# Attention stage of a one-layer language model block: q, k, v products in three f32r terms, and new orders of work on five engines

## Chip, cores and metric

The kernel runs on one core of a Trainium2 chip. The metric is device time in microseconds. Before the change it takes 3895.12 us, the median of three runs (3893.07 to 3898.6). The profiled execution took 3882.32 us, with a span of 3880.6 us from its first to its last instruction.

## What is computed

32 sequences of 512 tokens, width 256. Each token's row is an embedding plus a low-rank (LoRA) term. Then attention with 16 heads of 16: a local part (keys at most 64 positions away) and a global part (the first 64 keys), mixed by a gate. Then a mixture of 8 experts, two per token, with a capacity.

```python
h = take(emb, x) + 2.0 * take(lora_A.T, x) @ lora_B.T
n = layernorm(h)
q, k, v = split(n @ Wqkv + bqkv)              # 16 heads of 16
local  = softmax(q k^T / 4, |i - j| <= 64) v
glob   = softmax(q k[:64]^T / 4) v[:64]
gate   = sigmoid(n @ Wg + bg)
h = h + ((1 - gate) * local + gate * glob) @ Wout + bout
m = layernorm(h)                              # router, top 2 of 8, capacity
h = h + m + sum_k p_k * (silu(m @ w1[e_k]) @ w2[e_k])
```

The kernel computes the products for q, k and v in f32, and cuts q and k into bf16 terms for the scores.

## The kernel before

The kernel has a setup, an attention stage and an expert stage. The change lies in the setup and in the attention stage.

In the attention stage five engines each work through a list of their own, written out by hand as `ORDER["pe"]`, `["act"]`, `["dve"]`, `["pool"]` and `["sp"]`. An entry is (which sequence, stage, argument). The list of an engine is run once for each iteration i; "cur" is sequence i, "prev", "past" and "old" are i-1, i-2 and i-3, "nxt", "far" and "next" i+1, i+2 and i+3 (`REL`). So stages of five or six sequences lie between each other. Each engine works strictly in the order of its list; a stage begins by waiting for the semaphores of the stages whose results it needs. The small stages share two PSUM banks (`psX`), handed on in the order of TensorE's list (`take`): a stage waits until the reader of the last use of its bank is done.

The stages that matter here, of one sequence:

- "gather" 0 to 7 (POOL): eight indirect DMAs, alternately LoRA rows `la` (L582) and embedding rows `emb_t` (L585), 128 rows each. "scatter" 0 to 7 (POOL): eight indirect DMAs that write tokens' entries into the slot table (L592). These sixteen are all of POOL's indirect DMAs in a sequence.
- "scale1" (DVE) makes the normalized rows `xn`. "xn_t" 0, 1 (PE, L852) transposes them, four transposes each; ACT copies them to `xn_t` (L946).
- "qk" 0 to 3 (PE, L858): the products of `wqk` and `xn_t`, 512 columns, for two halves of the width. Each f32 matmul of the program is two instructions in the trace. ACT takes bf16 term one out of PSUM (L957), DVE the rest (L1123), ACT term two (L973), POOL term three ("qk3", L608).
- "qk_write" (SP) writes the terms to a scratch in DRAM, repeated; "load" 0 to 3 (SP, L658) brings a quarter of Q and K back, 4 heads at a time.
- "values" 0, 1 (PE, L795) and 2 (L800): the products for V of all tokens, and of the first 64.
- "max" 0 to 19 (PE, L699 to L721): scores against keys, whose row maxima DVE takes (L993, L997). There is one pair of PSUM banks for it, so max m+1 waits for DVE's reduction of max m. "m_rows", "m_out", "m_in" bring the maxima back as rows of Q.
- "exp" 0 to 19 (PE, L741, L748): the scores again, transposed; ACT takes exp (L903, L907). Also one pair of banks. "sel" (POOL, L568, L570) sets to zero what lies outside the band, for 16 of the 20.
- "out" (PE, L769, L774): probabilities times V; "evac" (ACT, L913); "mix" (PE transposes L817, DVE L1089 and L1096, POOL L601); "attn_t"; "project"; the second layernorm, the router and the ranks.
- "hold" (POOL, L620) adds the output bias to h; SP stores it and "hb" (SP, L662) loads it again.

In POOL's list of before, several indirect DMAs follow each other: `("next", "gather", 1), ("past", "scatter", 2), ("next", "gather", 2), ("next", "gather", 3), ("past", "scatter", 3), ("next", "gather", 4)` is one run, and there are three pairs.

## Time and profile before

| | |
|---|---|
| median of three runs | 3895.12 us |
| profiled execution | 3882.32 us, span 3880.6 us |
| mean granted TensorE clock | 0.952 |
| PE busy in the span | 3481.5 us (90%) |
| POOL busy | 2324.1 us (60%) |
| DVE busy | 2172.5 us (56%) |
| ACT busy | 1868.3 us (48%) |
| chain that ended last | PE 40%, all of it in the expert stage (L1462, L1497, L1437) |

PE is TensorE, with its weight loads apart (PEld); DVE is VectorE, ACT ScalarE, POOL GpSimd, SP the engine that issues most DMAs (its queue is SPq). L12 is line 12 of the kernel. A busy share is a mean over stages with different limits, so the windows of a stage say more. "PEclk" is the granted TensorE clock in a stretch, as a share of 2.4 GHz. In a timeline an entry in brackets is the idle time of the engine before the group, and what ended it: "issue" is time in which the engine waited for nothing that the profile shows, "remote" an event that none of the profiled engines gave. Durations of single matmuls contain the depth of their pipeline; how far apart they start is their cost in a row.

### The profile page before, as it was taken

To read this page: it belongs to the slowest core of one execution; us is meant where nothing else is said; L and a number is where in the kernel's file an instruction comes from. 1 tells how busy PE (TensorE), PEld (TensorE's weight loads), DVE (VectorE), ACT (ScalarE), POOL (GpSimd) and SP (SyncE) were. 2 spreads that over 40 slices of the span, in tenths; PEclk is the share of its full clock that TensorE was granted. 3 is DMA by queue.
4 is the path that set the end of the run, shared out by engine and by line. 5 is a ranking of instruction groups with operands and counts; after the bars stand their busy time and mean duration, and the time that the engine had idled before them with its cause. 6 is when DMAs were issued, how large, how long until landed. Compare 5 with 4: busy or idle time off the path is not lost. (4 is left out here: it accounts for less than half of the span.)

```text
span 3880.6 us, 117579 instructions
## 1 busy us (share of the span) xinstructions
PE 3481.5 (90%) x47537; PEld 2753.0 (71%) x47537; DVE 2172.5 (56%) x5392; ACT 1868.3 (48%) x3086; POOL 2324.1 (60%) x2599
## 2 busy tenths in 40 slices
PE   2898889888888888888899849999999999999998
PEld 1555555555555555555555539999999999999998
DVE  3576767767676776767677634343434344443333
ACT  0455555555555555555555624343444444444343
POOL 5566777777777777777776645444544444444443
PEclk7899999999999999999999969999999999999999
DMA  4354544445454444545454323232323233222222
GB/s 142 123 157 117 163 122 151 130 138 139 128 152 123 150 133 135 144 125 149 124 154 130 109 87 65 50 68 46 71 48 72 48 69 72 46 51 45 45 45 41
DMA packets 242540, 398.31 MB, mean 103 GB/s; under 512 B 34572, under 2 KB 150748, under 8 KB 242044
## 3 DMA queue, kind: packets, MB, share of 16 engines
q1 hardware_dynamic: 168540, 297.43, 25.0%
q0 software_dynamic: 70512, 91.16, 13.8%
q8 instruction: 345, 5.65, 0.6%
q10 hardware_dynamic: 3008, 2.95, 0.2%
q14 instruction: 135, 1.11, 0.1%
HBM read 198.55 MB, written 192.88 MB: 101 GB/s over the span
## 5 line engine op out<-in xcount | busy, mean ns | idle before, releaser
L1388 POOL DMA_INDIRECT out_y<-out_t,tok_out x264 | 425.7, 1612 | 747.3 <-DMA out_y<-out_t,tok_out 405.0
L1534 ACT ACTIVATE act<-psS 128x512 f32<-128x512 f32 x528 | 316.9, 600 | 882.1 <-PE psS L1462 880.9
L1596 DVE TENSOR_TENSOR h_lo<-act,h_hi 128x512 fp32r<-128x512 f32 x528 | 367.2, 695 | 562.3 <-ACT h_hi L1535 543.8
L993 DVE TENSOR_REDUCE negm<-psS 128x4 f32<-128x640 f32 x512 | 418.8, 818 | 452.3 <-remote 276.3
L903 ACT ACTIVATE pl<-psS 128x896 f32<-128x896 f32 x512 | 467.7, 913 | 379.9 <-PE psS L741 372.0
L568 POOL TENSOR_SCALAR_AFFINE_SELECT pl<-pl 128x512 f32<-128x512 f32 x512 | 354.3, 692 | 448.4 <-ACT pl L903 446.2
L1497 PE MATMUL psO<-w_hi,h_hi 128*128 128x256 f32 x2112 | 598.8, 284 | 0.8 <-DVE h_lo L1596 0.8
L1497 PE MATMUL psO<-w_lo,h_hi 128*128 128x256 f32 x2112 | 588.7, 279 | 0.0
L1497 PE MATMUL psO<-w_hi,h_lo 128*128 128x256 f32 x2112 | 587.6, 278 | 0.0
L1462 PE MATMUL psS<-xg_hi,w_hi 128*128 128x256 f32 x1984 | 551.7, 278 | 0.0
L1462 PE MATMUL psS<-xg_hi,w_lo 128*128 128x256 f32 x1984 | 551.5, 278 | 0.0
L1462 PE MATMUL psS<-xg_lo,w_hi 128*128 128x256 f32 x1984 | 551.3, 278 | 0.0
L1497 PEld LDWEIGHTS psO<-w_hi,h_hi 128*128 128x128 f32 x2112 | 397.0, 188 | 1.1 <-DVE h_lo L1596 1.0
L1497 PEld LDWEIGHTS psO<-w_lo,h_hi 128*128 128x128 f32 x2112 | 397.0, 188 | 0.0
L1497 PEld LDWEIGHTS psO<-w_hi,h_lo 128*128 128x128 f32 x2112 | 395.5, 187 | 0.0
L1462 PEld LDWEIGHTS psS<-xg_hi,w_hi 128*128 128x128 f32 x1984 | 375.1, 189 | 0.0
L1462 PEld LDWEIGHTS psS<-xg_lo,w_hi 128*128 128x128 f32 x1984 | 372.5, 188 | 0.0
L1462 PEld LDWEIGHTS psS<-xg_hi,w_lo 128*128 128x128 f32 x1984 | 372.4, 188 | 0.0
L699 PE MATMUL psS<-K,Q 96*32 96x160 bf16 (+2 forms) x8192 | 260.8, 237 | 105.7 <-DVE negm L993 71.2
L1628 DVE TENSOR_SCALAR out_t<-psO,wt_all 128x256 f32<-128x256 f32 x264 | 127.8, 484 | 360.7 <-PE psO L1497 355.8
L699 PEld LDWEIGHTS psS<-K,Q 96*32 96x32 bf16 x8192 | 165.6, 98 | 231.2 <-DVE negm L993 109.0
L570 POOL TENSOR_SCALAR_AFFINE_SELECT pl<-pl 128x512 f32<-128x512 f32 x512 | 328.0, 641 | 0.0
(232 smaller groups left out, 7728.6 us busy)
## 6 DMA issues: line engine op xcount, KB each, us to landing
qk_scr<-qk SPq DMA_DIRECT2D x64, 768.0 KB
Q<-qk_scr SPq DMA_DIRECT2D x128, 384.0 KB
K<-qk_scr SPq DMA_DIRECT2D x128, 384.0 KB
qk_scr<-qk SPq DMA_DIRECT2D x64, 512.0 KB
qk_scr<-qk SPq DMA_DIRECT2D x64, 256.0 KB
h_rows<-held SPq DMA_DIRECT2D x32, 512.0 KB
hb<-h_rows SPq DMA_DIRECT2D x32, 512.0 KB
x_rows<-x SPq DMA_DIRECT2D x32, 512.0 KB
```

The lines of the kernel that those rows point to most:

```text
L568: pool.affine_select(out=cols[:, :, 0:P], in_=cols[:, :, 0:P], compare_op=ALU.is_ge, fill=0.0, base=0, pattern=[[0, 4], [1, P]], channel_m ...
L570: pool.affine_select(out=cols[:, :, P:WIN], in_=cols[:, :, P:WIN], compare_op=ALU.is_ge, fill=0.0, base=0, pattern=[[0, 4], [-1, P]], chan ...
L699: pe.matmul(psS[SUB * c:SUB * (c + 1), 2 + a, q % 2 * BAND + lo:q % 2 * BAND + hi], Q[0:ROWS, 4 * g + 2 * v + a, (4 * q + c) * SUB:(4 * q ...
L903: act.activation(pl[:, v, half, :, lo:hi], psS[:, 0:2, lo:hi], ACT.Exp, scale=SCALE).then_inc(exp_done, 1)
L993: dve.tensor_reduce(negm[:, g, 0, v, :, 2 * half:2 * half + 2], psS[:, 2:4, 0:2 * BAND].rearrange("p a (q u) -> p a q u", u=BAND), AX.X, A ...
L1388: pool.indirect_dma_start(out=y[:, :], in_=out_t[:, tile.out, s, :], in_offset=None, out_offset=bass.IndirectOffsetOnAxis(ap=tok_out[:, ti ...
L1462: last = pe.matmul(psS[:, f // 2, (f % 2) * 256:(f % 2) * 256 + cols], w[:, tile.par, k, fs], x[:, k, 0:cols], start=(k == 0 and n == 0), ...
L1497: last = pe.matmul(psO[:, s, 0:D], h_[:, f, ts], w[:, tile.par, f, :], start=(f == 0 and n == 0), stop=(f == FT - 1 and n == 2))
L1534: act.activation(act32[:, b, :, 0:cols], src, ACT.Silu)
L1596: dve.tensor_tensor(h_lo[:, 2 * b:2 * b + 2, 0:cols], act32[:, b, :, 0:cols], h_hi[:, 2 * b:2 * b + 2, 0:cols].bitcast(F32), ALU.subtract) ...
L1628: dve.tensor_scalar(out_t[:, tile.out, s, :], psO[:, s, 0:D], wt_all[:, bass.ds(tile.h0 + s, 1)], None, ALU.mult).then_inc(out_done, 1)
```

## The change

1. The f32 products of q, k and v become sums of three f32r products: the operands are cut into a high part and the rest, and hi x hi, hi x lo and lo x hi are added up in PSUM. The weights are cut in the setup, by DVE. The transposed rows are cut for each sequence: ACT copies the high part out of PSUM, and a new stage "xn_lo" on DVE subtracts it from the PSUM tile. The bank is given free by DVE instead of ACT. "values" and "qk" wait for the low part.
2. The tiles of the cut rows have 64 columns more, a second copy of the first 64 tokens, so that values 2 is one product of 128 columns of tokens and 256 columns of weights instead of two half ones.
3. All five lists are written anew. In POOL's no two indirect DMAs follow each other, also not from one iteration to the next. The sixteen per sequence stay.

```diff
-        wv_sb = keep("wv_sb", [P, KT, D])
+        wv_hi = keep("wv_hi", [P, KT, D], F32R)
+        wv_lo = keep("wv_lo", [P, KT, D], F32R)
...
-        wqk = keep("wqk", [P, KT, 4, P])
+        wqk_hi = keep("wqk_hi", [P, KT, 4, P], F32R)
+        wqk_lo = keep("wqk_lo", [P, KT, 4, P], F32R)
...
+                    dve.tensor_copy(wv_hi[:, :, :], wv_raw[:, :, :])
                     for k in range(KT):
                         for s in range(2):
-                            dve.tensor_copy(wqk[:, k, 2 * s:2 * s + 2, :].rearrange("p a (d h) -> p a d h", d=HD),
-                                            wqk_raw[:, k, s * D:(s + 1) * D].rearrange("p (h a d) -> p a d h", a=2, d=HD))
+                            ins = dve.tensor_copy(wqk_hi[:, k, 2 * s:2 * s + 2, :].rearrange("p a (d h) -> p a d h", d=HD),
+                                                  wqk_raw[:, k, s * D:(s + 1) * D].rearrange("p (h a d) -> p a d h", a=2, d=HD))
+                    ins.then_inc(w_cut, 1)
+                    dve.wait_ge(w_cut, 1)
+                    dve.tensor_tensor(wv_lo[:, :, :], wv_raw[:, :, :], wv_hi[:, :, :].bitcast(F32), ALU.subtract)
+                    for k in range(KT):
+                        for s in range(2):
+                            dve.tensor_tensor(wqk_lo[:, k, 2 * s:2 * s + 2, :].rearrange("p a (d h) -> p a d h", d=HD),
+                                              wqk_raw[:, k, s * D:(s + 1) * D].rearrange("p (h a d) -> p a d h", a=2, d=HD),
+                                              wqk_hi[:, k, 2 * s:2 * s + 2, :].rearrange("p a (d h) -> p a d h", d=HD).bitcast(F32),
+                                              ALU.subtract)
...
-            xn_t = tmp("xn_t", [P, KT, T])
+            xn_hi = tmp("xn_hi", [P, KT, SIDE + T], F32R)
+            xn_lo = tmp("xn_lo", [P, KT, SIDE + T], F32R)
...
             ORDER["pe"] = (
...
-                ("nxt", "max", 9), ("nxt", "values", 0), ("nxt", "max", 10), ("prev", "logits", None), ("cur", "exp", 19),
-                ("nxt", "values", 1), ("cur", "out", 10), ("cur", "out", 11), ("nxt", "m_rows", 1), ("nxt", "values", 2),
-                ("nxt", "max", 11), ("far", "xn_t", 0), ("far", "xn_t", 1), ("nxt", "exp", 0), ("nxt", "max", 12), ("far", "qk", 0),
-                ("nxt", "exp", 1), ("far", "qk", 1), ("far", "qk", 2), ("nxt", "max", 13), ("far", "qk", 3), ("nxt", "exp", 2),
...
+                ("cur", "exp", 18), ("prev", "router", None), ("nxt", "max", 9), ("nxt", "values", 0), ("cur", "exp", 19),
+                ("nxt", "values", 1), ("cur", "out", 10), ("cur", "out", 11), ("prev", "logits", None), ("nxt", "m_rows", 1),
+                ("nxt", "max", 10), ("nxt", "values", 2), ("far", "xn_t", 0), ("far", "xn_t", 1), ("nxt", "exp", 0),
+                ("nxt", "max", 11), ("nxt", "exp", 1), ("far", "qk", 0), ("nxt", "max", 12), ("far", "qk", 1), ("nxt", "max", 13),
+                ("nxt", "exp", 2), ("far", "qk", 2), ("nxt", "max", 14), ("far", "qk", 3), ("nxt", "exp", 3), ("nxt", "max", 15),
+                ("cur", "mix", 0), ("nxt", "max", 16), ("nxt", "exp", 4), ("cur", "mix", 1), ("nxt", "out", 0), ("nxt", "max", 17),
+                ("nxt", "m_rows", 2), ("nxt", "exp", 5), ("cur", "mix", 2), ("nxt", "max", 18), ("nxt", "exp", 6),
+                ("nxt", "out", 1), ("nxt", "max", 19), ("nxt", "exp", 7), ("cur", "mix", 3), ("nxt", "exp", 8), ("nxt", "out", 2),
+                ("nxt", "out", 3), ("nxt", "exp", 9), ("prev", "ahead", None), ("cur", "attn_t", 0), ("far", "max", 0),
...
             ORDER["dve"] = (
...
+                ("nxt", "qk", 0), ("cur", "max", 13), ("nxt", "qk", 1), ("cur", "max", 14), ("nxt", "qk", 2),
...
+                ("past", "top", 6), ("far", "scale1", 3), ("nxt", "max", 10), ("far", "xn_lo", 0), ("far", "xn_lo", 1),
+                ("prev", "top", 0), ("nxt", "max", 11), ("prev", "top", 1), ("nxt", "max", 12),
...
             ORDER["pool"] = (
-                ("nxt", "hold", 0), ("far", "gather", 5), ("cur", "sel", 0), ("cur", "sel", 1), ("nxt", "hold", 1),
-                ("nxt", "qk3", 0), ("nxt", "qk3", 1), ("nxt", "qk3", 2), ("nxt", "qk3", 3), ("cur", "sel", 2), ("prev", "mix", 0),
-                ("cur", "sel", 3), ("old", "scatter", 4), ("old", "scatter", 5), ("prev", "mix", 1), ("cur", "sel", 5),
-                ("cur", "sel", 6), ("prev", "mix", 2), ("prev", "mix", 3), ("far", "gather", 6), ("cur", "sel", 7),
-                ("nxt", "hold", 2), ("cur", "sel", 8), ("far", "gather", 7), ("old", "scatter", 6), ("nxt", "hold", 3),
-                ("cur", "sel", 10), ("old", "scatter", 7), ("cur", "sel", 11), ("cur", "sel", 12), ("prev", "rstd2", None),
-                ("cur", "sel", 13), ("past", "scatter", 0), ("past", "scatter", 1), ("cur", "sel", 15), ("cur", "sel", 16),
-                ("cur", "sel", 17), ("next", "gather", 0), ("far", "rstd1", None), ("cur", "sel", 18), ("next", "gather", 1),
-                ("past", "scatter", 2), ("next", "gather", 2), ("next", "gather", 3), ("past", "scatter", 3), ("next", "gather", 4),
+                ("far", "gather", 4), ("nxt", "hold", 2), ("nxt", "hold", 3), ("far", "gather", 5), ("cur", "sel", 0),
+                ("old", "scatter", 0), ("cur", "sel", 1), ("far", "gather", 6), ("cur", "sel", 2), ("nxt", "qk3", 0),
+                ("nxt", "qk3", 1), ("nxt", "qk3", 2), ("nxt", "qk3", 3), ("prev", "mix", 0), ("cur", "sel", 3),
+                ("old", "scatter", 1), ("prev", "mix", 1), ("old", "scatter", 2), ("cur", "sel", 5), ("prev", "mix", 2),
+                ("cur", "sel", 6), ("far", "gather", 7), ("prev", "mix", 3), ("old", "scatter", 3), ("cur", "sel", 7),
+                ("old", "scatter", 4), ("cur", "sel", 8), ("old", "scatter", 5), ("cur", "sel", 10), ("old", "scatter", 6),
+                ("cur", "sel", 11), ("old", "scatter", 7), ("cur", "sel", 12), ("prev", "rstd2", None), ("cur", "sel", 13),
+                ("next", "gather", 0), ("cur", "sel", 15), ("cur", "sel", 16), ("next", "gather", 1), ("cur", "sel", 17),
+                ("far", "rstd1", None), ("cur", "sel", 18), ("next", "gather", 2), ("far", "hold", 0), ("next", "gather", 3),
+                ("far", "hold", 1),
...
             ORDER["sp"] = (
-                ("prev", "m_out", 3), ("cur", "load", 1), ("cur", "hold", None), ("prev", "m_in", 3), ("cur", "load", 2),
-                ("past", "x2", None), ("cur", "m_out", 0), ("cur", "m_in", 0), ("cur", "load", 3), ("cur", "m_out", 1),
-                ("nxt", "qk_write", (0, 0)), ("nxt", "qk_write", (0, 1)), ("nxt", "qk_write", (0, 2)), ("cur", "m_in", 1),
-                ("nxt", "qk_write", (1, 0)), ("nxt", "qk_write", (1, 1)), ("nxt", "qk_write", (1, 2)), ("nxt", "load", 0),
-                ("cur", "m_out", 2), ("past", "y", None), ("prev", "hb", None), ("cur", "m_in", 2),
+                ("old", "y", None), ("cur", "load", 1), ("prev", "m_out", 3), ("prev", "m_in", 3), ("cur", "m_out", 0),
+                ("cur", "load", 2), ("cur", "m_in", 0), ("nxt", "hold", None), ("prev", "hb", None), ("cur", "load", 3),
+                ("cur", "m_out", 1), ("cur", "m_in", 1), ("nxt", "qk_write", (0, 0)), ("nxt", "qk_write", (0, 1)),
+                ("past", "x2", None), ("nxt", "qk_write", (0, 2)), ("nxt", "qk_write", (1, 0)), ("nxt", "qk_write", (1, 1)),
+                ("nxt", "qk_write", (1, 2)), ("cur", "m_out", 2), ("nxt", "load", 0), ("cur", "m_in", 2),
...
-                            wv = wv_sb[:, :, :].rearrange("p k (v a d) -> p k a v d", a=2, d=HD)
-                            pe.wait_ge(xn_t_done, KT * (s + 1))
+                            pe.wait_ge(xn_lo_done, KT * (s + 1))
                             take(key, v_done, 3 * s + arg + 1)
                             if arg < 2:
                                 for j in range(2):
-                                    tok = slice((2 * arg + j) * P, (2 * arg + j + 1) * P)
+                                    tok = slice(SIDE + (2 * arg + j) * P, SIDE + (2 * arg + j + 1) * P)
                                     for k in range(KT):
-                                        last = pe.matmul(psX[:, b, j * D:(j + 1) * D], xn_t[:, k, tok], wv_sb[:, k, :],
-                                                         start=(k == 0), stop=(k == KT - 1))
+                                        for n, (x_, w) in enumerate(((xn_hi, wv_hi), (xn_hi, wv_lo), (xn_lo, wv_hi))):
+                                            last = pe.matmul(psX[:, b, j * D:(j + 1) * D], x_[:, k, tok], w[:, k, :],
+                                                             start=(k == 0 and n == 0), stop=(k == KT - 1 and n == 2))
                             else:
                                 for k in range(KT):
-                                    for a in range(2):
-                                        last = pe.matmul(psX[64 * a:64 * (a + 1), b, 0:P], xn_t[:, k, 0:64], wv[:, k, a, :, :],
-                                                         start=(k == 0), stop=(k == KT - 1))
+                                    for n, (x_, w) in enumerate(((xn_hi, wv_hi), (xn_hi, wv_lo), (xn_lo, wv_hi))):
+                                        last = pe.matmul(psX[:, b, 0:D], x_[:, k, 0:2 * SIDE], w[:, k, :],
+                                                         start=(k == 0 and n == 0), stop=(k == KT - 1 and n == 2))
...
                         if stage == "xn_t":
                             pe.wait_ge(xn_done, QB * (s + 1))
-                            take(key, xn_t_done, KT * s + arg + 1)
+                            take(key, xn_lo_done, KT * s + arg + 1)
...
                         if stage == "qk":
-                            pe.wait_ge(xn_t_done, KT * (s + 1))
+                            pe.wait_ge(xn_lo_done, KT * (s + 1))
                             take(key, qk_rest_done, 4 * s + arg + 1)
                             for k in range(KT):
-                                last = pe.matmul(psX[:, b, :], wqk[:, k, arg, :], xn_t[:, k, :],
-                                                 start=(k == 0), stop=(k == KT - 1))
+                                for n, (w, x_) in enumerate(((wqk_hi, xn_hi), (wqk_hi, xn_lo), (wqk_lo, xn_hi))):
+                                    last = pe.matmul(psX[:, b, :], w[:, k, arg, :], x_[:, k, SIDE:SIDE + T],
+                                                     start=(k == 0 and n == 0), stop=(k == KT - 1 and n == 2))
...
-                            act.activation(xn_t[:, arg, :], psX[:, b, :], ACT.Copy).then_inc(xn_t_done, 1)
+                            act.activation(xn_hi[:, arg, 0:SIDE], psX[:, b, 0:SIDE], ACT.Copy)
+                            act.activation(xn_hi[:, arg, SIDE:SIDE + T], psX[:, b, :], ACT.Copy).then_inc(xn_hi_done, 1)
...
+                        if stage == "xn_lo":
+                            dve.wait_ge(xn_hi_done, KT * s + arg + 1)
+                            if arg == 0:
+                                need(dve, v_ready, 3 * s)
+                                need(dve, qk_ready, 4 * s)
+                            x_ = psX[:, BANK["xn_t", arg, s], :]
+                            dve.tensor_tensor(xn_lo[:, arg, 0:SIDE], x_[:, 0:SIDE], xn_hi[:, arg, 0:SIDE].bitcast(F32), ALU.subtract)
+                            dve.tensor_tensor(xn_lo[:, arg, SIDE:SIDE + T], x_, xn_hi[:, arg, SIDE:SIDE + T].bitcast(F32),
+                                              ALU.subtract).then_inc(xn_lo_done, 1)
```

## Rows read from the trace of the kernel before

**Rows 1.** windows by stage: us; busy PE, PEld, DVE, ACT, POOL; clock; DMA share, GB/s.

```profile
333.20:2091.60 1758.40, 1559.27 (x27784) 971.25 (x27773) 1225.34 (x3300) 966.21 (x1506) 1270.18 (x1637) 0.95 0.48 138
2400.00:3880.00 1480.00, 1450.81 (x12479) 1448.68 (x12477) 594.26 (x1169) 627.73 (x1150) 686.30 (x521) 0.99 0.30 54
```

**Rows 2.** DMA issues of one tile: count, durations, first and last start.

```profile
L662 SPq DMA_DIRECT2D hb<-h_rows x11: 441/452/2097, 1012.4 to 1688.7; - x11
...
L668 SPq DMA_DIRECT2D x_rows<-x x32: 360/376/381, 225.2 to 2265.0; - x32
```

**Rows 3.** timeline of PE, from 1109 us: start, duration, line, operation, [idle before].

```profile
1109.92 0.46 PE L699 MATMUL psS<-K,Q 96*32 96x96 bf16 x16
...
1110.43 0.33 PE L878 MATMUL psX<-ident,score_t 128*128 128x128 f32 x1
...
1115.19 0.66 PE L800 MATMUL psX<-wv_sb,xn_t 128*64 128x128 f32 x8
...
1117.99 0.24 PE L715 MATMUL psS<-mask,identb 128*32 128x128 bf16 x2 [1.16 <-issue]
...
1120.85 1.08 PE L852 MATMUL psX<-ident,xn 128*128 128x128 f32 x4 [0.96 <-issue]
```

**Rows 4.** timeline of POOL, first and last of a run of six indirect DMAs.

```profile
1112.33 1.03 POOL L585 DMA_INDIRECT emb_t<-in_L_tok_emb_weight,id_cur  x1 [0.18 <-issue]
...
1118.86 0.98 POOL L582 DMA_INDIRECT la<-lora_rows,id_cur  x1 [0.30 <-issue]
```

**Rows 5.** timelines of DVE and ACT, the first work behind that run.

```profile
1122.47 0.83 DVE L993 TENSOR_REDUCE negm<-psS 128x4 f32<-128x640 f32 x1 [7.96 <-remote]
...
1120.15 0.56 ACT L924 ACTIVATE V<-psX 64x128 f32<-64x128 f32 x2 [2.96 <-remote]
```

**Rows 6.** a window at 1124 us, and PE's timeline of the q,k products.

```profile
1124.20:1127.80 3.60, 3.60 (x13) 1.24 (x13) 0.82 (x1) 0.70 (x2) 1.22 (x2) 0.54 0.00 0
...
1124.21 3.60 PE L858 MATMUL psX<-xn_t,wqk 128*128 128x512 f32 x4
...
1128.13 3.70 PE L858 MATMUL psX<-xn_t,wqk 128*128 128x512 f32 x8
```

**Rows 7.** timelines of POOL and PE around two of the pairs.

```profile
1100.47 0.98 POOL L592 DMA_INDIRECT slot_table<-entry,slot_i  x1 [0.30 <-issue]
...
1100.24 0.45 PE L699 MATMUL psS<-K,Q 96*32 96x160 bf16 x15
...
1101.99 1.06 PE L774 MATMUL psO<-pg,V 128*32 128x512 f32 x8
...
1156.85 0.46 PE L699 MATMUL psS<-K,Q 96*32 96x96 bf16 x16 [1.06 <-DVE negm L993]
```

**Rows 8.** timelines of POOL and PE, two single DMAs, the last q,k, the first max.

```profile
1108.81 1.02 POOL L582 DMA_INDIRECT la<-lora_rows,id_cur  x1 [0.28 <-POOL id_cur L577]
...
1148.92 0.99 POOL L582 DMA_INDIRECT la<-lora_rows,id_cur  x1
...
1132.26 1.98 PE L858 MATMUL psX<-xn_t,wqk 128*128 128x512 f32 x4
...
1150.67 0.46 PE L699 MATMUL psS<-K,Q 96*32 96x96 bf16 x16 [0.52 <-DMA K<-qk_scr]
```

**Rows 9.** timeline of PE, a values group.

```profile
1108.02 1.97 PE L795 MATMUL psX<-wv_sb,xn_t 128*128 128x256 f32 x8
```

**Rows 10.** groups by line, 1000 to 1700 us, and DVE's timeline in the setup.

```profile
L1144 DVE TENSOR_TENSOR h<-psX,hb 128x512 f32<-128x512 f32 x20 | 13.6, 680 | 0.0
...
L924 ACT ACTIVATE V<-psX 64x128 f32<-64x128 f32 x20 | 5.5, 273 | 20.7 <-remote 20.6
...
42.09 1.26 DVE L316 COPY wqk<-wqk_raw 128x256 f32<-128x256 f32 x4
```

**Rows 11.** groups by line, whole run: count, busy, mean ns, idle before.

```profile
L769 PE MATMUL psO<-pl,V 128*32 128x256 f32 x2048 | 184.2, 385 | 6.2 <-POOL pl L570 2.5 <-issue 1.5
...
L699 PE MATMUL psS<-K,Q 96*32 96x96 bf16 x1024 | 136.3, 212 | 68.2 <-DVE negm L993 43.9 <-DMA K<-qk_scr 15.9 <-issue 7.0
```

More of the change, by code:

```diff
@@ L481, in build @@
-                ("nxt", "exp", 1), ("far", "qk", 1), ("far", "qk", 2), ("nxt", "max", 13), ("far", "qk", 3), ("nxt", "exp", 2),
-                ("nxt", "max", 14), ("cur", "mix", 0), ("nxt", "exp", 3), ("nxt", "out", 0), ("nxt", "max", 15), ("cur", "mix", 1),
-                ("nxt", "exp", 4), ("nxt", "max", 16), ("cur", "mix", 2), ("nxt", "exp", 5), ("nxt", "max", 17), ("nxt", "out", 1),
-                ("nxt", "m_rows", 2), ("nxt", "exp", 6), ("nxt", "max", 18), ("cur", "mix", 3), ("nxt", "exp", 7),
@@ L485, in build @@
-                ("nxt", "max", 19), ("nxt", "out", 2), ("nxt", "exp", 8), ("nxt", "out", 3), ("prev", "ahead", None),
-                ("cur", "attn_t", 0), ("far", "max", 0), ("cur", "attn_t", 1), ("nxt", "m_rows", 3), ("nxt", "exp", 9),
+                ("cur", "exp", 11), ("prev", "project", 1), ("nxt", "max", 3), ("cur", "out", 4), ("cur", "exp", 12),
+                ("far", "embed", None), ("nxt", "max", 4), ("cur", "exp", 13), ("cur", "out", 5), ("far", "lora", 0),
+                ("cur", "exp", 14), ("far", "lora", 1), ("nxt", "max", 5), ("cur", "out", 6), ("cur", "exp", 15), ("cur", "out", 7),
@@ L520, in build @@
-                ("prev", "top", 6), ("far", "max", 4), ("next", "lora", 0), ("far", "cut", (0, 0)), ("cur", "scale2", 0),
+                ("nxt", "qk", 0), ("cur", "max", 13), ("nxt", "qk", 1), ("cur", "max", 14), ("nxt", "qk", 2),
+                ("cur", "cut", (2, 0)), ("nxt", "qk", 3), ("cur", "max", 15), ("cur", "cut", (2, 1)), ("prev", "mix", (0, 0)),
+                ("cur", "cut", (2, 2)), ("prev", "mix", (0, 1)), ("cur", "cut", (2, 3)), ("past", "top", 2), ("cur", "max", 16),
+                ("prev", "mix", (1, 0)), ("prev", "mix", (1, 1)), ("past", "top", 3), ("cur", "max", 17), ("cur", "kg", 2),
@@ new lines, in build @@
+                ("past", "top", 4), ("cur", "kg", 3), ("prev", "mix", (2, 0)), ("cur", "max", 18), ("prev", "mix", (2, 1)),
+                ("nxt", "zgate", 0), ("old", "rank", 5), ("prev", "mix", (3, 0)), ("prev", "mix", (3, 1)), ("cur", "max", 19),
+                ("cur", "cut", (3, 0)), ("cur", "cut", (3, 1)), ("far", "la_cut", 0), ("cur", "cut", (3, 2)), ("past", "rank", 0),
+                ("cur", "cut", (3, 3)), ("nxt", "max", 0), ("past", "rank", 1), ("past", "rank", 2), ("far", "la_cut", 1),
```

68 lines of the change are left out of this document (30 added, 38 removed).

## The prediction, made before the change was run

> **What bounds the kernel now.** I read the windows by stage first, then one sequence's timeline on each engine. The windows part the 90% for which TensorE (PE) is busy into two stages [rows 1]: the expert stage from 2400 us on, where PE is busy 1450.8 of 1480 us at clock 0.99 and which the change doesn't touch, and the attention stage, where PE is busy 88.7% at clock 0.95, GpSimd (POOL) 72%, VectorE (DVE) 70%, ScalarE (ACT) 55%. The whole gain or loss is made in attention. There one sequence takes 67.6 us: ten repeats of one DMA lie between 1012.4 and 1688.7; over all 32 the same kind of count gives (2265.0 - 225.2)/31 = 65.8 [rows 2], the ends being thinner.
>
> In this loop PE is the fullest engine, but it isn't full. Reading its timeline from 1115 us [rows 3]: the groups from values 2 (1115.19) to the first q,k product (1124.21) take 9.0 us. They are values 2, two max groups, two sets of transposes and one score group. A max group undisturbed takes 0.5 (1109.92 to 1110.43, first two rows); by sizes I put the others at 0.6, 0.6, 0.6 and 0.4, 3.2 in all. So 5.8 us are lost, in gaps called "issue" even inside the max group, where nothing is waited for. At that time POOL runs six indirect DMAs with nothing between them, 1112.33 to 1119.84, and a seventh after one addition [rows 4]. DVE's next max begins at 1122.47 after 7.96 us idle, though its matmuls ended by 1118.23; ACT sat 2.96 us until 1120.15 with its input done at about 1115.9; both are put down to "remote", no engine's event [rows 5]. So while indirect DMAs follow each other, signals between the other engines arrive late, for all of them at once.
>
> The idle time also costs clock. From 1124.20 to 1127.80 the granted clock is 0.54, that is nearly all at the lower level of 1.2 GHz, after PE had been half idle for 5 us; four q,k instructions then take 3.53 us, and eight at 1.00 take 3.70 [rows 6]. Lost: 3.53 - 1.77 = 1.8 us. The mean 0.95 of the stage says that it happens in each sequence.
>
> Pairs do the same on a small scale [rows 7]: beside the second DMA at 1100.47 a max group runs from 1100.24 to 1101.99, 1.75 for 0.5, lost 1.2. Of the other two pairs one costs a wait of 1.06 (at 1156.85) and the last, read in the same way, about 0.3. DMAs that stand alone: three besides the seventh. Beside the one at 1108.81 PE loses nothing (its values group of 1108.02 takes 1.97 us, as the other one does), beside that of 1148.92 it waits 0.52 [rows 8, 9], the third costs about 0.2. Sum per sequence: 5.8 + 1.8 for the run, 2.6 for three pairs, 0.7 for three single ones.
>
> **The change part by part.**
>
> *Product passes.* Each f32 matmul is two instructions. Sixteen for q,k at (3.70 - 0.16)/8 = 0.44, the 0.16 being the tail of the last, 7.1 us at full clock; for values 16 at 1.97/8 = 0.246, 3.9 us, and 0.6 for values 2 [rows 6, 9]. After: 24 f32r instructions of 512 columns for q,k, 24 of 256 columns for values 0 and 1, 6 of 256 for values 2. The expert stage gives f32r with 256 columns: 12479 instructions in 1450.8 us, 0.116 each [rows 1], so 0.23 for 512 at most and 0.21 if part of the 0.116 is fixed; I take 0.22: 5.3, 2.8 and 0.7, with 0.1 to start each of seven groups 9.5 us against 11.6. Saved 2.1 us; the ends are 1.7 and 2.8 (no start cost). I take 2.5, nearer the upper end, since the groups of before carry their start cost too.
>
> *Extra cuts.* ACT copies two times 64 columns more; nearest row 0.27 (64x128), 0.5 us on an engine 55% busy: no cost. DVE gets two subtractions of 128x512 out of PSUM, like 0.68, and two of 64 columns, 0.2 each, at most the 0.27 of the ACT row [rows 10]: 1.8 us on DVE, 47.1 to 48.9 us busy, still under PE. What costs is latency: q,k now waits for transposes, ACT and DVE in a row. From the last transpose: 0.6 + 0.2 on ACT, 0.7 + 0.2 on DVE, some 0.1 of signals, 1.8 us; PE has a score, a max and a score group of 1.3 us between. I take 0.5 us of waiting, ends 0 and 1.9 (no cover). Behind the subtractions DVE holds max 11, so PE's max 12 is next in danger, but q,k work of PE lies before it. The PSUM bank of the transposes comes free later by the same time; inside the 0.5.
>
> *The lists.* The order changes on all five engines; the same 16 indirect DMAs per sequence now always have a sel, a mix or another POOL operation between them. This takes away the run and the pairs: 5.8 + 1.8 + 2.6 = 10.2, and with the 0.7 of the single ones 10.9. It adds 16 single ones. Their price is the crux: the trace has 0, 0.5 and 0.2, and half a pair is 0.43. I take 0.35, 5.6 us; ends 0 and 0.65 (a DMA of 1.0 us and some 0.4 behind it, until PE and DVE start again [rows 5, 7], make 1.4 in which a signal is late by 0.7 on average, felt nearly in full). On POOL the gap before a DMA goes from 0.30 behind a DMA to 0.18 behind a sel, nothing on the path. With no long idle left the clock should stay up.
>
> *Moved DMAs.* SP's q,k writes and loads keep their order, y and hold move to the other side of the loads. PE's wait for K at the first max of a quarter is 15.9 us over all 32 sequences, 0.5 each [rows 11]. Between q,k 3 and max 0 PE's new list holds twelve score and max groups of about 0.45 and eight mix and output groups of about 1, some 14 us with the small ones; now 16.4 pass there (1134.2 to 1150.67 [rows 8]), and the wait at the end is 0.52. With the delays of five single DMAs and the earlier start of q,k 0 it comes out about even. Cost 0 to 1.5, taken 0, since y moved out of its way.
>
> *Setup.* DVE gets a copy of 128x512, a subtraction of that size and four of 128x256 strided; like copies take 1.26/4 = 0.3 each [rows 10]: 3 us, in the open, as POOL's first gathers begin only after DVE's last. Ends 1.5 and 4.
>
> Sum: 67.6 - 10.9 + 5.6 - 2.5 + 0.5 = 60.3 us a sequence, 7.3 less. 26 full periods give 190; the five thinner intervals at the ends, at half, 18; setup -3: 205 us. The profiled execution took 3882.3 us (span 3880.6 and 1.7 around it) and would take 3677; the median shown, 3895.1, lies 12.8 above it, so 3690.
>
> *A rule against it.* ACT and DVE are held while POOL issues indirect DMAs [rows 4, 5]. The Trainium skill, "SBUF — State Buffer", section "SBUF: two separate sides", says that engine ports and DMA ports are disjoint, and that PE, ACT and DVE's own ports never wait on anyone; only DVE and GpSimd share a lock. By it a run of DMAs delays no other engine, the waits have another source, and new lists bring nothing: a rival, below. The rows speak against it by coincidence in time, which isn't yet cause.
>
> **The rivals.**
>
> *Single ones are nearly free* (0.05 each). For: 1108.81. Then 60.3 - 4.8 = 55.5 us, 12.1 less: 26 x 12.1 + 30 - 3 = 342, and 3553. Against: POOL needs about 49 us busy and 16 x 0.2 of gaps in 55.5, in order; it would become the bound at about 57, which gives 3590.
>
> *The delay is the DMAs' in sum, or isn't theirs.* If each single costs 0.65, the loop is 65.1; if only the passes count, 67.6 - 2.5 + 0.5 = 65.6. Saved 2.2: 26 x 2.2 + 6 - 3 = 60, and 3835. For: each DMA is still issued and the traffic (DMA share 0.48) stays. Against: delays of 5 us at the run and 1 at a pair, on three engines.
>
> *POOL's order becomes the bound, slower.* Some twelve DMAs that ran in bunches now stand between sels, and each pushes the next sel back by 1.17 us. PE's output group waits for sel, ACT's exp for the output group's release. If these waits are felt in full, 12 x 1.17 = 14.0, and the loop is 67.6 - 10.9 - 2.5 + 0.5 + 14.0 = 68.7; that is 1.1 x 28.5 + 3 = 34 slower, 3930. It decides once PE waits for pl from POOL at nearly every output group. Against: that wait is 2.5 us in all now [rows 11], POOL has 19 us idle a sequence.
>
> **How the numbers follow.** Forecast 0.52 (own range 3620 to 3760: singles 0.15 to 0.5, passes 1.7 to 2.8), singles free 0.20, in sum or not theirs 0.19, slower 0.09, of which 0.01 within 0.2% of before, which is about what this kernel's measurement can tell from no change. Hence faster 0.91, same 0.01, slower 0.08. Predicted 3690; the range 3580 to 3840 takes in the first rival at POOL's bound and the middle of the second.
>
> **What would show it.** Right: a sequence in 58 to 63 us; no idle of DVE over 2 us put down to "remote"; granted clock about 1.00 in attention; q,k instructions 0.22 apart; PE waits of 0 to 0.6 near single DMAs. Wrong: clock still 0.95; waits of over 2 us with no DMA behind another; POOL idle under 4 us a sequence with PE waiting for pl; DVE's waits for the new cut over 1 us.

## The result: 87 us faster where 205 were forecast

The changed kernel takes 3806.7 us (3804.0 to 3807.8) against 3894.1 (3884.0 to 3898.6): ratio 0.9778, 95% interval 0.9758 to 0.9798. The forecast was 3690, range 3580 to 3840.

The windows of the changed kernel (us; busy PE, PEld, DVE, ACT, POOL; clock; DMA share, GB/s), to be set beside [rows 1]:

```profile
333.00:2050.00 1717.00, 1482.93 (x28561) 1035.89 (x28557) 1296.36 (x3449) 983.97 (x1575) 1294.30 (x1659) 0.94 0.47 142
2310.00:3790.00 1480.00, 1463.81 (x12612) 1461.76 (x12611) 598.21 (x1177) 634.62 (x1163) 690.39 (x525) 1.00 0.30 55
```

PE is busy 86.4% of attention, less than before, and the clock is 0.94, not 1.00. The repeats of one DMA, as in [rows 2]:

```profile
L680 SPq DMA_DIRECT2D hb<-h_rows x11: 446/453/1726, 1022.9 to 1671.1; - x11
...
L686 SPq DMA_DIRECT2D x_rows<-x x32: 359/1041/2654, 255.5 to 2195.3; - x32
```

A full sequence takes 64.8 us instead of 67.6, where 60.3 were forecast; over all 32 it is 62.6 instead of 65.8. What DVE's maxima waited for, of the kernel before (total us, times):

```profile
  remote: 276.3, 57
  PE psS L715: 175.9, 173
```

and of the changed one:

```profile
  PE psS L733: 183.3, 206
  PE psS L739: 16.3, 36
```

As forecast, none of DVE's idle before its maxima is called "remote" any more; shorter delays are left and are measured below. But PE's groups by line, as in [rows 11], have a wait for K that was 15.9 us before (line L699 there) and is 84.9 now, 13.4 and 13.6 of it a single wait at the start:

```profile
L717 PE MATMUL psS<-K,Q 96*32 96x160 bf16 (+2 forms) x8192 | 262.6, 239 | 105.2 <-DMA K<-qk_scr 84.9 <-DVE negm L1013 14.1 <-DVE negm L1017 1.2
```

DVE waits for the last gather of the sequence two ahead (waits by line: total, times, longest):

```profile
DVE la_four L1189 <- DMA emb_t<-in_L_tok_emb_weight,id_cur: 141.0, 32, 12.9
```

One sequence's timeline shows both waits meeting:

```profile
1096.73 0.39 PE L877 MATMUL psX<-xn_hi,wqk_lo 128*128 128x512 f32 x1
...
1110.58 0.32 SPq L676 DMA_DIRECT2D Q<-qk_scr  x1
1110.95 0.71 SPq L676 DMA_DIRECT2D K<-qk_scr  x1
1111.18 1.00 POOL L603 DMA_INDIRECT emb_t<-in_L_tok_emb_weight,id_cur  x1 [0.15 <-issue]
...
1116.18 0.73 PE L717 MATMUL psS<-K,Q 96*32 96x96 bf16 x16 [2.53 <-DMA K<-qk_scr]
1116.64 0.63 DVE L1189 CAST la_four<-la 128x128 fp32r<-128x128 f32 x1 [3.65 <-DMA emb_t<-in_L_tok_emb_weight,id_cur]
...
1118.03 1.09 PE L842 MATMUL psX<-ident,attn 128*128 128x128 f32 x4 [0.92 <-DVE ahead L1076]
1119.15 0.60 ACT L955 ACTIVATE attn_t<-psX 128x512 f32<-128x512 f32 x1 [4.38 <-issue]
...
1120.76 2.94 PE L849 MATMUL psX<-wout_sb,attn_t 128*128 128x256 f32 x8
```

The last q,k product ends at 1097.1 (first row). Load 0 is issued 13.5 us later, and max 0 starts 19.1 later; before, max 0 started 16.4 behind that product [rows 8]. SP's list accounts for a part of the first: m load 1 now stands ahead of the q,k writes and waits for its own write, the residual's store stands among them:

```profile
1096.92 0.26 SPq L657 DMA_DIRECT2D Q<-m_scr  x1
1097.37 0.92 SPq L667 DMA_DIRECT2D qk_scr<-qk  x2
1098.33 1.07 SPq L686 DMA_DIRECT2D x_rows<-x  x1
1099.44 5.44 SPq L667 DMA_DIRECT2D qk_scr<-qk  x4
```

SP's waits for such a write of m, of the kernel before and of the changed one (total, times, longest):

```profile
SPq L639 <- DMA m_scr<-m_t: 113.0, 59, 4.4
```

```profile
SPq L657 <- DMA m_scr<-m_t: 277.8, 95, 7.6
```

After these waits the clock falls, in a new place:

```profile
1110.00:1116.00 6.00, 3.17 (x37) 1.17 (x29) 2.89 (x6) 3.07 (x5) 5.49 (x8) 0.99 0.75 192
1116.00:1124.00 8.00, 6.91 (x110) 5.41 (x114) 4.62 (x17) 1.92 (x3) 4.96 (x7) 0.58 0.49 146
1118.00:1121.00 3.00, 2.97 (x51) 2.47 (x52) 1.51 (x7) 1.84 (x3) 0.92 (x1) 0.50 0.50 118
```

PE is half idle for 6 us, then the granted clock is at its lower level, 1.2 GHz.

### The profile page after: what moved, and what is told of

Same layout as the page of the kernel before. It is cut to its first block and busy times, and to the rows that moved or that the text cites. A ratio compares the mean times of both kernels' runs of the same rounds, so it can differ in the third digit from the quotient of the medians.

```text
span 3806.0 us, 118732 instructions
## 1 busy us (share of the span) xinstructions
PE 3366.0 (88%) x47985; PEld 2813.8 (74%) x47985; DVE 2243.9 (59%) x5526; ACT 1874.0 (49%) x3150; POOL 2331.6 (61%) x2599
## 5 line engine op out<-in xcount | busy, mean ns | idle before, releaser
L1417 POOL DMA_INDIRECT out_y<-out_t,tok_out x264 | 426.6, 1616 | 745.5 <-DMA out_y<-out_t,tok_out 403.2
L586 POOL TENSOR_SCALAR_AFFINE_SELECT pl<-pl 128x512 f32<-128x512 f32 x512 | 329.1, 643 | 320.3 <-ACT pl L922 316.7
L717 PE MATMUL psS<-K,Q 96*32 96x160 bf16 (+2 forms) x8192 | 262.6, 239 | 105.2 <-DMA K<-qk_scr 84.9
L588 POOL TENSOR_SCALAR_AFFINE_SELECT pl<-pl 128x512 f32<-128x512 f32 x512 | 328.5, 642 | 0.0
```

The costliest lines, as they stand in the source:

```text
L586: pool.affine_select(out=cols[:, :, 0:P], in_=cols[:, :, 0:P], compare_op=ALU.is_ge, fill=0.0, base=0, pattern=[[0, 4], [1, P]], channel_m ...
L588: pool.affine_select(out=cols[:, :, P:WIN], in_=cols[:, :, P:WIN], compare_op=ALU.is_ge, fill=0.0, base=0, pattern=[[0, 4], [-1, P]], chan ...
L717: pe.matmul(psS[SUB * c:SUB * (c + 1), 2 + a, q % 2 * BAND + lo:q % 2 * BAND + hi], Q[0:ROWS, 4 * g + 2 * v + a, (4 * q + c) * SUB:(4 * q ...
L1417: pool.indirect_dma_start(out=y[:, :], in_=out_t[:, tile.out, s, :], in_offset=None, out_offset=bass.IndirectOffsetOnAxis(ap=tok_out[:, ti ...
```

## The experiments

They ran on two groups of chips. The changed kernel, E1 to E4 and E5 to E8 met chips on which the kernel before takes 3892 to 3894 us: the *late* chips. E9 to E12 and the three sets behind them met chips on which the same kernel takes 3678, 3684 and 3681 us: the *prompt* chips. Each ratio is to the kernel before on the same chip. All the late sets were taken before the prompt ones, so whether it is the chip or the hour was not settled. The stage behind attention takes the same on both: from SP's last store of a sequence's rows (`x_rows`) to the end, the kernel before needs 1616 us in its late trace and 1619 in its prompt one, so the 209 us by which these traces differ lie ahead of it.

**E1, products alone**, in the lists of before:

```diff
+ three-term f32r products, 64 columns more
  ORDER["dve"]: ... ("nxt","max",11), ("far","xn_lo",0), ("far","xn_lo",1), ("nxt","max",12) ...
```

> The three-term products alone, in the lists of before (the two low-part stages stand on DVE behind max 11). Theory A, the passes give 2.5 us a sequence where PE is the bound but the long run of indirect DMAs still holds all engines: a sequence goes from 67.6 to about 66 us, 40 to 70 us less, 3825 to 3855; DVE's idle of 7 to 8 us put down to remote stays, clock 0.95. Theory B, the whole gain of the change was the passes and the lists give nothing: 3800 to 3815.

Measured: 3893.4, ratio 1.0002 (0.9992 to 1.0012). Both expectations missed. In the trace PE waits 0.6 us a sequence for DVE's low part; its idle called "issue" at the transposes, which now also wait for DVE's release of the bank, is 56.5 us in all where it was 30.2; DVE's maxima behind the run of six start 5.7 us late (median) where they started 4.3 late; and the clock of attention is 0.93 instead of 0.95.

**E2, the five new lists alone**, f32 products (the new lists, without "xn_lo"):

> The five new lists alone, with the f32 products of before and without the low-part stages. Theory A, spacing the DMAs removes about 9 us of waiting a sequence and a new chain, from the q,k writes over the load of K to the next first max, takes most of it back: 3840 to 3870, with PE's wait for K at 2 to 3 us a sequence. Theory B, the lists give nothing: 3885 to 3900.

Measured: 3838.2, 0.9859 (0.9830 to 0.9887), just under Theory A's range, but not by its mechanism: PE's wait for K is 22.3 us in all, 0.3 a sequence without the first wait, not 2 to 3. DVE's wait for the gather is there, 112.7 us in all. The products on top bring 31 us, to 3807.

**E3, POOL's list alone spaced**, all else as before:

```diff
-  past.scatter 0, past.scatter 1, sel 15, sel 16, sel 17, gather 0, rstd1, sel 18, gather 1, past.scatter 2, gather 2, gather 3, past.scatter 3, gather 4
+  past.scatter 0, sel 15, past.scatter 1, sel 16, gather 0, sel 17, gather 1, rstd1, past.scatter 2, sel 18, gather 2, (next) hold 0, gather 3, sel 0, old.scatter 3 ...
```

> The kernel before with POOL's list alone changed, so that no two indirect DMAs follow each other; products and the other four lists are those of before. Theory A, a run of indirect DMAs delays the signals between all engines until it ends, a single one by at most 1.5 us: the delays of 4 to 5 us at DVE's max go, none over 1.5 us is left, the low clock in each sequence goes, and a sequence takes 60 to 63 us, 3680 to 3770 in all. Theory B, the cost is that of 16 DMAs however they stand: 3870 to 3910. In between (3780 to 3860): the delays go as in A, and a chain of DMAs takes over as in the changed kernel.

Measured: 3783.1, 0.9721 (0.9701 to 0.9741). The longest delay of a maximum is 1.27 us, as Theory A had it, but the time lies above its range and the clock of attention is 0.97, not 1.00; the new wait for K of the changed kernel isn't there (13.4 us in all, 13.0 of it at the start). One list does more than the whole change. So the other four lists, with the products, cost.

**E4, gathers off POOL**, the kernel before with the eight gathers as plain DMAs from fixed rows on SP's queue (so other rows are gathered); pairs of scatters stay:

```diff
-  pool.indirect_dma_start(out=la[:, q, :], in_=lora_rows[:, :], in_offset=at)
+  sp.dma_start(la[:, q, :], lora_rows[row:row + P, :])
```

> The kernel before with the eight gathers of a sequence taken off POOL: SP issues plain DMAs of the same sizes from fixed rows instead, so the embedding rows are not those of the tokens, and the routing differs. Eight scatters stay, in four pairs. Theory A, it is POOL's indirect DMAs in a row that delay signals: the run shrinks to a pair, no delay over 2.3 us, a sequence about 60 us, attention 200 us shorter (the expert stage may differ by the routing and is left out of the comparison). Theory C, the traffic on the DMA engines delays the signals, whoever issues it: delays of 4 us stay where the gathers now stand, and attention is at most 50 us shorter.

Measured: 3639.9, 0.9354 (0.9339 to 0.9370). Attention, from the first sequence's store to the last one's, is 246 us shorter (1794 against 2040), where Theory C allowed 50. The same bytes move: the loss is not traffic. Not all of the 246 need be delays, since POOL also has eight instructions less in a sequence; E12 bears on that.

**E5, E6, E7, the two new waits**, in the changed kernel. E5 is the SP edit, E6 the DVE edit, E7 both:

```diff
-  m_out 1, m_in 1, qk_write (0,0), qk_write (0,1), x2, qk_write (0,2), (1,0), (1,1), (1,2)
+  m_out 1, qk_write (0,0), qk_write (0,1), m_in 1, qk_write (0,2), (1,0), (1,1), (1,2), x2
```

```diff
-  cut (3,1), far.la_cut 0, cut (3,2), rank 0, cut (3,3), max 0, rank 1, rank 2, far.la_cut 1
+  cut (3,1), cut (3,2), rank 0, cut (3,3), max 0, rank 1, rank 2, far.la_cut 0, far.la_cut 1
```

> The changed kernel with SyncE's list alone reordered: the layer's m load 1 goes behind the first two q,k writes, and the store of the residual behind all q,k writes. Theory A (the new period is set by a chain that the new SyncE order delays: q,k writes, then load of K): the matmuls on K wait under 1 us a sequence for it instead of 2.6, load 0 is issued 3 to 5 us earlier, and the time comes to 3740 to 3790. Rival (the K wait only shows the place where another lateness surfaces; ScalarE or VectorE bound the period): the wait moves to VectorE's or ScalarE's rows and the time stays within 0.5% of 3807.

> The changed kernel with VectorE's list alone reordered: the cut of the next sequence's gathered rows that waits 4.3 us for its gather goes behind the rank step. Theory A (period set by the K chain): VectorE's wait of 4.3 us on the gather goes, but TensorE still waits for K, so 0 to 40 us are gained: 3765 to 3807. Rival (VectorE's standing still there is what makes the period longer): 4.3 us over 25 sequences less some slack, 3710 to 3760.

> Both reorderings of the changed kernel at once (SyncE's writes ahead of m load 1 and the residual's store; VectorE's cut behind the rank step). Theory A: the two waits are one after the other in time on TensorE's path, so the gains add to more than either alone: 3690 to 3770, the half-speed stretch of each sequence gone or under 4 us. Rival (something else in the new lists holds the period): within 20 us of the better of the two alone.

Measured: E5 3802.3 (0.9769, 0.9752 to 0.9785), E6 3771.1 (0.9701, 0.9672 to 0.9730), E7 3706.9 (0.9522, 0.9507 to 0.9538). Alone 4 and 36 us, together 100: the waits overlap in time. With either left something still waits there (PE's wait for K is 52.4 us in all in E5 and 111.2 in E6; DVE's for the gather 138.3 in E5), and the clock of attention is 0.95 and 0.96. In E5 SP's waits for m's write fell from 277.8 to 94.7 us. E5 met its rival's figure, E6 and E7 Theory A's. E7's window, and its wait for K:

```profile
333.00:2050.00 1717.00, 1529.10 (x30393) 1060.35 (x30392) 1387.22 (x3659) 1047.73 (x1674) 1361.33 (x1749) 0.99 0.51 149
```

```profile
L718 PE MATMUL psS<-K,Q 96*32 96x160 bf16 (+2 forms) x8192 | 248.3, 234 | 80.7 <-DMA K<-qk_scr 47.1 <-DVE negm L1014 26.4 <-DVE negm L1018 1.2
```

Clock 0.99, and 3707 where the prediction said 3690. That agreement hides two errors of opposite sign, as the last runs show: more than forecast from the delays, nothing from the products.

**E8, products with E3's spaced list**, low part made behind max 11:

> The kernel before with the three-term products and with GpSimd's list alone spaced (SyncE, ScalarE, TensorE and VectorE lists as before, except that the low part of the normalised rows is made behind the eleventh maximum). Theory A (products are worth their shorter passes where no run of indirect DMAs stands behind them): the spaced list alone gave 3783, less 1 to 2.5 us over 32 sequences, 3700 to 3755. Rival (products give nothing in the lists of before, as alone: the extra step of VectorE for the low part takes what the passes give): 3770 to 3800.

Measured: 3803.1, 0.9762 (0.9742 to 0.9782), that is 20 us above E3. Worse than the rival's range: with POOL's list spaced and the rest as before the products cost, where in E1 they gave nothing. PE waits 38.1 us in all, 1.1 a sequence, for the low part.

**E9 to E12**, all from E7: E9 with f32 products; E10 with POOL's list bunched (`gather 1, 2, 3, 4, 5, scatter 0` in one run, scatters 1-2, 3-4, 5-6 in pairs); E11 with two moves in PE's list (m_rows 0 behind max 8, max 0 behind attn_t 1), the first followed in ACT's; E12 with gathers on SP as in E4.

> The lists of the last experiment that took 3706.9 (both reorderings), with the products of the kernel before (one f32 matmul for each pair of operands instead of three f32r ones, no low part of the rows made on VectorE). If the shorter passes of the products are worth the 2.5 us a sequence of the prediction once the waits beside them are gone: 3707 + 2.5 x 32 = 3787, say 3770 to 3800. Rival (they are worth what they gave in the new lists as they stood, 31 us, or nothing as in the lists of before): 3705 to 3745.

> The lists that took 3706.9, with GpSimd's alone changed: its indirect DMAs stand in one run of six, three pairs and four singles, as in the kernel before. Theory A (a run of six costs 7.6 us, three pairs 2.6, singles 0.35 each): 6 us a sequence more, 3870 to 3900. Rival (most of what the whole change gave came of other places in the lists, and a run costs only what the slack of TensorE doesn't take): 3720 to 3780.

> The lists that took 3706.9, with TensorE's list changed in two places: the first quarter's rows of maxima are turned behind maximum 8 (they wait 1.06 us a sequence for VectorE's cut), and maximum 0 stands behind both turns of the attention's output (it waits 1.09 us for K); ScalarE's list follows the first. If the two waits are on the path: 2 us over some 30 sequences less, 3645 to 3680. Rival (VectorE's maxima bound the period by then, so the waits come back under its name): 3695 to 3715.

> The lists that took 3706.9, with the eight gathers of a sequence taken from GpSimd and made plain DMAs from fixed rows on SyncE's queue (the rows gathered are therefore not the reference's); GpSimd keeps the eight single scatters. If singles cost 0.35 us each, as the prediction has it: 2.8 us a sequence, 3600 to 3635. Rival (singles are hidden in TensorE's slack): 3690 to 3707. Rival (SyncE's queue is late by its new DMAs): above 3710.

Measured, on a prompt chip (before 3678.4): E9 3681.8 (1.0015, 0.9998 to 1.0032), E10 3768.0 (1.0244, 1.0216 to 1.0273), E11 3670.8 (0.9981, 0.9961 to 1.0002), E12 3580.3 (0.9741, 0.9714 to 0.9768). No expected time can be read against these, as all were worked out from 3707 on a late chip. So the comparison was made again on one chip, with these expectations:

> The changed kernel again, on one chip with the three runs that follow. Two kinds of chip were met: on the first the kernel before takes 3892 to 3895 us and signals come up to 5 us late behind GpSimd's indirect DMAs; on the second it takes 3678 and they hardly do. On the first kind: ratio 0.978 again. On the second, if the gain came from the spacing of the indirect DMAs alone: the new waits (K, the gather's cut) are left, so not faster, ratio 1.00 to 1.02; rival (the gain has nothing to do with the delay): 0.97 to 0.985 there too.

> The changed kernel with both reorderings again, as the one that the next two runs are set beside. First kind of chip: 0.952 again. Second kind: the rest of its lists is level with the lists of before, 0.99 to 1.00.

> The same lists with the f32 products of before. If the shorter passes are worth 2.5 us a sequence once the two waits are gone: 1.02 times m_e7 (3787 where that is 3707). Rival (they are worth nothing to 31 us, the extra steps on VectorE taking the rest): 1.000 to 1.008 times m_e7.

> The same lists with GpSimd's indirect DMAs in one run of six, three pairs and four singles. Where signals are late behind them (first kind of chip): 6 us a sequence more, 1.043 to 1.052 times m_e7, by the prediction's terms. Second kind: only what the later gathers cost, which the one run there put at 3768 against 3671 to 3682 for lists with singles, so 1.01 to 1.03 times m_e7. Rival (the delay costs nothing in these lists): the same 1.01 to 1.03 on the first kind.

A prompt chip again (before 3683.8): the change 3770.5, ratio 1.0230 (1.0180 to 1.0281), so slower, though not surely by 2%, and above both expected ranges; E7 3683.6 (0.9997, 0.9975 to 1.0019), as expected; E9 3682.7 (0.9999, 0.9979 to 1.0020); E10 3770.8 (1.0240, 1.0189 to 1.0291). So in E7's lists the products are worth 0 (E9 against E7: the rival), and with the delays absent a bunched order can still lose: in E10 PE waits for K 4.3 us a sequence, and its ratio to E7, 1.024, lies in the range expected for prompt chips. What bunching costs E7 on a late chip wasn't measured.

**The kernel before, and E3, once more:**

> The kernel before itself, for its trace on one chip with the next run. Second kind of chip (3670 to 3690 us): VectorE's maxima start within 0.1 us of TensorE's end even beside the run of six, where they came 4.3 us late on the first kind; a sequence takes 6 to 7 us less than the 65.8 of the first. First kind: 3890 to 3900 and delays of 4 to 5 us. Ratio 1.000 either way.

> The kernel before with GpSimd's list alone spaced (no two indirect DMAs behind one another), again. If the gain of 0.972 on the first kind came of the delays behind a run: on the second kind 0.995 to 1.010. Rival (the spaced order is better by itself, whatever the signals do): 0.97 to 0.985 there too. First kind: 0.972 again.

A prompt chip (before 3681.3): 3675.5 (0.9979, 0.9953 to 1.0006) and 3713.9 (1.0100, 1.0064 to 1.0136). Both as expected for prompt chips, the second at the edge of its range. Spacing is worth 2.8% on a late chip and costs 1.0% here. What DVE's maxima wait for in the kernel before, on this chip, beside the 276.3 above:

```profile
  PE psS L715: 202.3, 193
  PE psS L721: 21.4, 28
  remote: 4.6, 2
```

and its run of six, the same code as in [rows 3 to 5]:

```profile
1142.46 0.95 POOL L585 DMA_INDIRECT emb_t<-in_L_tok_emb_weight,id_cur  x1 [0.30 <-issue]
...
1143.60 0.28 PE L715 MATMUL psS<-mask,identb 128*32 128x128 bf16 x7
1143.72 1.01 POOL L592 DMA_INDIRECT slot_table<-entry,slot_i  x1 [0.30 <-issue]
...
1143.96 0.82 DVE L993 TENSOR_REDUCE negm<-psS 128x4 f32<-128x640 f32 x1 [2.25 <-PE psS L715]
1145.03 0.98 POOL L582 DMA_INDIRECT la<-lora_rows,id_cur  x1 [0.30 <-issue]
...
1147.95 3.70 PE L858 MATMUL psX<-xn_t,wqk 128*128 128x512 f32 x8
```

DVE starts 0.08 us behind PE's last matmul (1143.60 + 0.28), beside the fifth DMA of the run; in [rows 5], also beside the fifth, it came 4.2 us late. POOL's DMAs last as long as there, and lie as close. What differs in these rows is when DVE sees PE's signal. Over the window from 400 to 2000 us it starts at most 0.2 us late beside a run of six (50 maxima).

## Why the prediction was wrong

**Each late signal's price.** Beside each kernel its time on a late and a prompt chip. Their difference is taken for what the delays cost it; that rests on two comparisons, the equal stage behind attention and the signals that are prompt in the prompt traces, and nothing else was held against it:

| | late | prompt | delays |
|---|---|---|---|
| before | 3893 | 3681 | 212 |
| E3, POOL's list spaced | 3783 | 3714 | 69 |
| the change | 3807 | 3770 | 37 |
| E7, both moves | 3707 | 3684 | 23 |

*Mechanism and run.* "Signals between the other engines arrive late" was right for PE's signals to DVE and ACT. From 400 to 2000 us, where PE's last matmul ended beside an indirect DMA or less than 0.5 us behind it, DVE's maxima start after PE's end by 4.27 us (median) at a run of six, 2.11 at a pair, 0.34 at a single in the change and 1.24 in E3, and with no DMA near by 0.04 to 0.06; ACT's exponentials by 1.39 at a pair and 0.53 at a single. The two figures for singles differ by where PE ends: within 0.25 us of the DMA's start DVE is 1.25 late (25 cases in E3), about 1.0 behind it 0.49 (48 in the change), 2.0 behind it 0.05 (16 in E3). So a signal seems to be held until some 1.5 us behind the start of the last DMA, an estimate from these three rows. On prompt chips all medians are under 0.2.

*The prices* were both too high. The prediction's 26 full periods and 5 halves are 28.5 sequences. Taking away 10.9 us in each would be 311; all delays of before cost 212, 7.4 a sequence. Singles at 5.6 would be 160; they cost 37, 0.08 each (69 in E3, 0.15). Net the term was forecast at 151 and measured at 212 - 37 = 175: within 24 us, by errors that cancel. 1108.81 [rows 8], at which PE lost nothing, was the typical one.

*The step that failed* is "Moved DMAs ... Cost 0 to 1.5, taken 0, since y moved out of its way". On prompt chips, where no delay is in play, the change is 87 us slower than before, and E7's two moves give these 87 back: 3 us a sequence. On late chips the same two moves give 100. The prediction looked at y and hold and not at m load 1 and the residual's store, which came ahead of the writes, and not at all at la_cut, which came to stand some 2 us behind its gather's issue, where the gather lands 5.5 behind it (1111.18 to 1116.64). Its upper end, 1.5, held only half of the cost. That is 87 of the 118 us that are missing. The wait for K that it took as 0.5 a sequence was misread too, for all but 2.5 us of it is one wait at the start:

```profile
PE psS L699 <- DMA K<-qk_scr: 15.9, 5, 13.4
```

```profile
PE psS L717 <- DMA K<-qk_scr: 84.9, 31, 13.6
```

The new lists have one more wait that no term had and no experiment took away: PE waits for ACT's exponentials 50.5 us in all in the change, 5.1 before.

*The second step that failed* is "Product passes ... I take 2.5". The passes did get shorter: q,k instructions start 0.23 apart (0.22 forecast). This stretch is at full clock:

```profile
1094.29 0.40 PE L877 MATMUL psX<-xn_hi,wqk_hi 128*128 128x512 f32 x1
1094.53 0.39 PE L877 MATMUL psX<-xn_lo,wqk_hi 128*128 128x512 f32 x1
1094.76 0.40 PE L877 MATMUL psX<-xn_hi,wqk_lo 128*128 128x512 f32 x1
```

But E7 and E9, on one chip, with three-term and f32 products, PE busy 1532 and 1564 of 1717 us:

```profile
333.00:2050.00 1717.00, 1532.20 (x30540) 1072.59 (x30533) 1403.23 (x3685) 1054.31 (x1690) 1369.84 (x1759) 0.97 0.51 149
```

```profile
333.00:2050.00 1717.00, 1563.98 (x30138) 1008.43 (x30137) 1372.05 (x3593) 1047.18 (x1637) 1374.86 (x1765) 0.99 0.51 149
```

and the two kernels' waits of the maxima's matmuls:

```profile
L718 PE MATMUL psS<-K,Q 96*32 96x160 bf16 (+2 forms) x8192 | 255.4, 237 | 96.8 <-DMA K<-qk_scr 74.8 <-DVE negm L1014 15.8 <-DVE negm L1018 1.5
```

```profile
L702 PE MATMUL psS<-K,Q 96*32 96x160 bf16 (+2 forms) x8192 | 247.7, 233 | 64.9 <-DVE negm L996 30.2 <-DMA K<-qk_scr 28.3 <-DVE negm L1000 1.5
```

PE's busy time fell by 1.1 us a sequence (31.8 us over the 29 sequences of the window), or by 1.8 if the time at 1.2 GHz is counted at half (1542 to 1490 us), so the passes gave nearly what was forecast, and a lower clock, 0.97 against 0.99, took 0.7 of it. The wait for K rose by 46.5 us, 1.5 a sequence: PE's work wasn't the bound there; what the shorter passes freed came out as a longer wait for K. It isn't the low part that holds K up. From the last transpose to the first q,k product pass 2.0 us in E7 and 1.9 in E9 (medians), 0.1 for the term of 0.5, and the products themselves take 8.1 instead of 9.4. But from their end to SP's load 0 pass 12.3 us instead of 9.5: the last q,k write begins 4.7 behind them instead of 3.6, and SP waits for the landing of these writes 101.3 us in all instead of 60.0. Why that stretch grew isn't shown. The prediction priced latency against PE's cover at that spot alone, not against the load at the end of the chain. Net forecast: 2.0 a sequence less, 57 us; measured 0 in these lists, and 31 us in those of the change (E2 against the change, late chips).

*The clock.* "With no long idle left the clock should stay up" fell with the first step: an idle did come back. In E7 it is 0.99 on a late chip, as forecast, and 0.97 on a prompt one.

*Sum.* Forecast: 151 for the delays, 57 for the passes with the low part, 0 for the chain, -3 for the setup: 205. Measured: 175, and 0 for the passes, -87 for the chain (the setup in these two): 88, where the times differ by 87. This sum can't fail, as its terms are differences of the same four times; what the runs show is each term. E2 parts the 87 in another way, on late chips alone: the lists gave some 55 where 151 were forecast, the products with their setup 31 where 54 were. By either account most of what is missing was lost in the lists.

*The rivals.* "Single ones are nearly free" was right for its price (0.05 forecast, 0.05 to 0.15 measured), and didn't show in the time. "POOL's order" didn't happen: PE waits 12.1 us in all for pl, 2.6 before. "The delay isn't theirs" is ruled out on late chips: E3 gained 2.8% there by POOL's order alone. It stood on the rule of the Trainium skill, "SBUF — State Buffer", section "SBUF: two separate sides", that PE, ACT and DVE's own ports never wait on anyone. On prompt chips delays are under 0.2 us. The rule is on ports, these delays are of signals, and their cause isn't shown by any run.

*Left open:* why chips differ; why E12's gathers on SP still gain 2.6% where signals are prompt (fewer instructions on POOL, fixed rows, and a wait for K of 0.43 us a sequence went together), which means that a part of E4's gain may not be delays either; and E10 on a late chip.

## What to carry to other kernels

When a list is written anew, follow every chain that crosses queues, write to load to first use, position by position, before pricing what the new list removes: here two entries took back half of the gain. An engine's shorter work is worth nothing where a chain through other engines and DMAs sets the period; ask what the change does to that chain, up to the load at its end. And a gain that rests on a delay should be measured on more than one chip: this change is 2.2% faster on some and 2.3% slower on others, where E7 is 4.8% faster and level.

## What the runs showed of the hardware

The same kernel takes 3893 or 3681 us. On the late chips PE's signals come late to DVE beside GpSimd's indirect DMAs, by 4.3 us at six (5.7 in E1), 2.1 at two and 0.3 (the change) or 1.2 (E3) at one, and to ACT by 1.4 at two and 0.5 at one, all medians; on the others by less than 0.2. Plain DMAs on SP's queue don't do it: in E4, on a late chip, the maxima beside no indirect DMA start at most 0.14 us late.

In the change, E5 to E7, E9 and E10 PE waits 1.03 to 1.07 us a sequence for a small operation of DVE. In E7, late chip:

```profile
1114.49 0.18 DVE L1037 TENSOR_TENSOR m_cut<-m_rest,m_cut 128x32 bf16<-128x32 f32 x1
...
1146.83 0.66 POOL L587 TENSOR_SCALAR_AFFINE_SELECT pl<-pl 128x512 f32<-128x512 f32 x1
1147.05 1.66 DVE L1037 TENSOR_TENSOR m_cut<-m_rest,m_cut 128x32 bf16<-128x32 f32 x1
1147.42 0.65 POOL L589 TENSOR_SCALAR_AFFINE_SELECT pl<-pl 128x512 f32<-128x512 f32 x1
```

Nine times its length, beside three selects of POOL (a third begins at 1148.01). The Trainium skill, "SBUF — State Buffer", section "SBUF: two separate sides", says that a DVE operation with two SBUF inputs and a GpSimd operation that reads SBUF lock each other out; this row agrees, though no run took the selects away. E11 took that wait off PE's list and gained nothing that can be measured against E7 (0.9981 and 0.9997 of before): its wait for K stayed, and PE waited for DVE's maxima instead, 1.7 us a sequence.
